# Two deformable convolutions turned from unrolled half images into a loop over tile rows, with smaller patches in the second

## The reference, cut to what matters

```
off1 = conv2d(x, w_off1, b_off1)                      # 18 channels: (dy, dx) of 9 taps
out  = relu(bn(deform_conv(x, off1, w_dc1, stride 1, pad 2, dilation 2)))
off2 = conv2d(out, w_off2, b_off2)
out  = relu(bn(deform_conv(out, off2, w_dc2, 1, 2, 2)) + x)

deform_conv: for every tap (ky, kx) and pixel (r, c)
    ys = r - 2 + 2*ky + dy,   xs = c - 2 + 2*kx + dx
    sample = bilinear value of the image at (ys, xs), zero outside
    out   += w_dc[:, :, ky, kx] @ sample
```

## Time and profile before

| what | us |
|---|---|
| median of 3 runs | 894.47 |
| profiled execution | 889.64 |
| its span | 887.6 |
| PE matmul busy | 728.3 (82%) |
| DVE busy | 484.3 (55%) |
| ACT busy | 417.0 (47%) |

### The profile page before, as it was taken

The page is one execution under the profiler, slowest core; times in us unless marked ns, Lnnn a source line. Parts: engine busy times, 40 slices in busy tenths (PEclk is TensorE's granted clock), DMA queues, the critical chain, the costliest instruction groups (busy, mean ns, idle before and its releaser), DMA issues.

```text
span 887.6 us, 40461 instructions
## 1 busy us (share of the span) xinstructions
PE 728.3 (82%) x18746; PEld 567.3 (64%) x18746; DVE 484.3 (55%) x840; ACT 417.0 (47%) x830; POOL 161.4 (18%) x190
## 2 busy tenths in 40 slices
PE   6787877788767887778788656999999999999546
PEld 2355555566633455555566545999999999998433
DVE  0565554455604645446455564666666666666654
ACT  1665455554315554546544143445445445545442
POOL 7000000000030000000000153343443443341300
PEclk8889878866769798887976578999999999999669
DMA  5400000000004000000000170000000000000002
GB/s 171 82 4 5 4 4 5 5 4 4 5 6 81 4 5 4 4 4 4 5 4 4 29 193 1 1 2 1 0 0 0 0 0 0 0 0 0 0 1 96
DMA packets 7835, 16.58 MB, mean 19 GB/s; under 512 B 1982, under 2 KB 5950, under 8 KB 7286
## 3 DMA queue, kind: packets, MB, share of 16 engines
q1 hardware_dynamic: 7678, 14.21, 6.3%
HBM read 10.34 MB, written 3.87 MB: 16 GB/s over the span
## 4 chain that ended last, share of the span: by engine, by line
PE 76%; issue 10%; DVE 6%; ACT 5%; POOL 1%; DMA 1%; SPq 0%; DVEq 0%
PE banks L227 20%; PE banks L145 14%; PE banks L696 7%; PE banks L680 7%; PE banks L726 6%; PE banks L458 4%; PE banks L737 4%; PE banks L716 3%; PE banks L691 2%; PE banks L180 2%; PE banks L166 2%; PE banks L707 2%; ACT hx L273 1%; DVE norm_stats L629 1%; ACT hy L278 1%
## 5 line engine op out<-in xcount | busy, mean ns | idle before, releaser
L227 PE MATMUL banks<-s,y 32*64 32x96 f32 (+9 forms) x10752 | 191.1, 268 | 66.0 <-issue 65.9
L318 DVE TENSOR_TENSOR s<-hy,hx 128x384 f32<-128x384 f32 (+3 forms) x336 | 144.4, 476 | 183.4 <-PE banks L227 181.8
L227 PEld LDWEIGHTS banks<-s,y 32*64 32x64 f32 x10752 | 160.2, 154 | 109.9 <-issue 100.2
L145 PE MATMUL banks<-w_dc,tiled 64*32 64x192 f32 x3584 | 130.2, 412 | 20.3 <-issue 13.7
L268 ACT COPY y<-banks 128x384 f32<-128x384 f32 x192 | 81.8, 484 | 114.0 <-PE banks L145 114.0
L145 PEld LDWEIGHTS banks<-w_dc,tiled 64*32 64x32 f32 x3584 | 74.3, 131 | 53.8 <-issue 26.6
L794 ACT COPY hy<-banks 128x512 f32<-128x512 f32 x64 | 37.6, 588 | 116.7 <-PE banks L726 116.7
L278 ACT ACTIVATE hy<-banks 128x512 f32<-128x512 f32 (+2 forms) x144 | 72.9, 583 | 38.4 <-PE banks L180 38.3
L898 POOL TENSOR_TENSOR y<-y,stats 128x1024 f32<-128x1024 f32 x33 | 62.8, 1902 | 142.2 <-DVE stats L839 142.2
L273 ACT ACTIVATE hx<-banks 128x384 f32<-128x384 f32 x144 | 61.4, 505 | 31.8 <-PE banks L166 23.9
L680 PE MATMUL banks<-src,s 128*128 (+1 forms) x560 | 75.0, 279 | 1.1 <-ACT src L617 1.1
(11 more groups left out here) (137 smaller groups left out, 876.9 us busy)
## 6 DMA issues: line engine op xcount, KB each, us to landing
src<-in_x_dram SPq DMA_DIRECT2D x4, 578.0 KB, 5.5
y<-in_w_dram SPq DMA_DIRECT2D x1, 2080.0 KB
off<-in_w_dram SPq DMA_DIRECT2D x2, 1024.0 KB
out_dram<-tokens SPq DMA_DIRECT2D x4, 512.0 KB, 2.6
offsets_dram<-tokens SPq DMA_DIRECT2D x32, 54.0 KB
off<-offsets_dram SPq DMA_DIRECT2D x16, 108.0 KB
w_dc<-in_w_dc_dram SPq DMA_DIRECT2D x2, 288.0 KB, 6.0
y<-in_w_attn_dram SPq DMA_DIRECT2D x1, 512.0 KB, 4.9
```

The costliest lines, as they stand in the source:

```text
L145: last = nc.tensor.matmul(m.ps[32 * j:32 * j + 32, FIRST_BANK + (count + g) % RING, (col % 2) * 192:(col % 2) * 192 + 192], m.tiled[rows, ...
L227: last = nc.tensor.matmul(out[:, r0:r0 + strip.n, first:first + width], m.y[32 * j:32 * j + 32, g, (s // 3) % 2 * Y_SLOTS + strip.slot, co ...
L318: nc.vector.tensor_tensor(dst, hy, hx[:, :, r0:r0 + strip.n, :], ALU.mult).then_inc(cv.s_ready, 1)
```

## The change

- TensorE's sampler becomes a loop (`pe.Fori(0, TR)`) of 8 iterations, one per source tile row. The body has the 9 taps written out; each with one x item, one y item, 32 sample matmuls, and in six taps (0, 4, 5, 6, 7, 8) one w item behind the samples. The other engines stay unrolled in the same order. Waits in the loop are against `i * constant + constant`, and the coordinate matmuls read `m.off_flat` at an address that moves with i.
- The four output banks hold 12 rows (OUT_ROWS). After a tile row ScalarE copies the rows that are new (`copied`), VectorE adds the overlap to the sums in `tokens` (`added`), TensorE clears the banks (4 matmuls of 384 columns) and goes on. Batch norm and ReLU are applied per tile row (`rows_act`, `rows_dve`), the last two rows at the end (`last_act`, `last_dve`).
- Column hats are computed for the 4 new rows only and kept in `hx_near` for the next tile row; one x item is 4 matmuls (128 and 64 or 32 columns), all 128 partitions deep (`near_sel`), one y item is 2 matmuls of 8 or 6 rows of 32.
- A w item is emptied by one copy of 768 elements in place of two of 384; x and y items likewise by one activation.
- GpSimd stages one tile row at a time (`stage_pool`, 4 copies a row) and cuts the whole image only for the far sampler.
- `REACHES = [2, 1]`: patches of 8x12 in the first convolution and 6x10 in the second, whose flag is compared with 1.
- VectorE makes s in two instructions per tap: over the old rows (2 * reach) and the 4 new ones. SLOTS goes from 5 to 3.
- Both halves of the offsets are awaited at the sampler's start.

```diff
-REACH = 2
+REACHES = [2, 1]
-SLOTS = 5
+SLOTS, HY_SLOTS = 3, 3
+OUT_ROWS = 12
+FIRST_WEIGHTED = [("w", ky, part, 0) for ky in range(3) for part in range(2)][0:5]
+FIRST_COORDS = [("x", tap, -1) for tap in range(3)] + coords(0) + coords(1) + [("x", tap, -1) for tap in range(3, 6)]
+AHEAD = 2
+STEP_WEIGHTED = {0: (2, 1, 0), 4: (0, 0, 1), 5: (0, 1, 1), 6: (1, 0, 1), 7: (1, 1, 1), 8: (2, 0, 1)}
+def columns_near(nc, m, cv, k, tap, row, n, i=None):
+    _, cols, ahead = window(cv)
+    kx = tap % 3
+    for late in range(2):
+        wide = 2 * cv.reach if late else TILE_COLS
...
+        for g in range(2):
...
+            last = nc.tensor.matmul(dst[:, :, :, TILE_COLS * late:TILE_COLS * late + wide],
+                                    m.near_sel[:, 6 + ((ahead * 3 + kx) * 2 + late) * 2 + g, :], src[:, :, :, 0:wide],
+                                    start=True, stop=True, skip_group_check=True)
+    last.then_inc(cv.filled, 1)
 def sampler_pe(nc, pe, m, cv):
+    for half in range(HALVES):
+        pe.wait_ge(cv.moved[half], MOVES)
+    for k, item in enumerate(FIRST_COORDS, len(FIRST_WEIGHTED)):
...
+    with pe.Fori(0, TR) as i:
+        k = BEFORE_LOOP
+        for t in range(TAPS):
+            later, tap = divmod(t + AHEAD, TAPS)
+            pe.wait_ge(cv.emptied, i * PER_ROW + (k - 1))
+            columns_near(nc, m, cv, k, tap, new_rows(cv, tap) + TILE_ROWS * later, TILE_ROWS, i)
+            k += 1
+            pe.wait_ge(cv.emptied, i * PER_ROW + (k - 1))
+            rows_near(nc, m, cv, k, tap, first_row(cv, tap) + TILE_ROWS * later, i)
+            k += 1
+            if t == 0:
+                pe.wait_ge(cv.copied, i + COPIED_FROM)
+                pe.wait_ge(cv.added, i + (ADDED_FROM - 1))
+                pe.wait_ge(cv.cleared, 1)
+                for bank in range(PAIRS):
+                    nc.tensor.matmul(m.ps[:, bank, 0:OUT_ROWS * W], m.zeros[:, 0:P], m.zeros[:, 0:OUT_ROWS * W],
+                                     start=True, stop=True, skip_group_check=True)
+            if t in STEP_WEIGHTED:
+                pe.wait_ge(cv.emptied, i * PER_ROW + (k - 1))
+                if STEP_WEIGHTED[t] == (0, 0, 1):
+                    pe.wait_ge(cv.staged, i * PAIRS + 2 * PAIRS)
...
+            pe.wait_ge(cv.s_ready, i * (2 * TAPS) + (2 * t + 2))
+            for col in range(TC):
+                first, width, skip = near_columns(cv, col, kx)
+                for j in range(4):
+                    for g in range(2):
...
+                        last = nc.tensor.matmul(out[:, r0:r0 + n, first:first + width],
+                                                m.yk[32 * j:32 * j + 32, ky, g, col, kx * C:(kx + 1) * C],
+                                                s_rows(m, cv, t)[32 * j:32 * j + 32, :, g, at:at + width],
+                                                start=False, stop=True, skip_group_check=True)
+            last.then_inc(cv.sampled, 1)
+            if t in STEP_WEIGHTED:
+                weighted_near(nc, m, cv, k, *STEP_WEIGHTED[t][0:2])
+                k += 1
 def sampler_act(nc, act, m, cv):
...
+    for tile_row in range(TR):
+        for t in range(TAPS):
+            if t == 2 and tile_row >= 2:
+                cv.rows_act(act, tile_row - 2)
+            for kind, *_ in step_items(tile_row, t):
+                if t == TAPS - 1 and kind == "w" and tile_row < TR - 1:
+                    act.wait_ge(cv.sampled, TAPS * (tile_row + 1))
+                    first, n = (TILE_ROWS, 2 * TILE_ROWS) if tile_row == 0 else (2 * TILE_ROWS, TILE_ROWS)
+                    at = TILE_ROWS * (tile_row - 1) + first
+                    nc.scalar.copy(sum_rows(m, at, n), out_rows(m, first, n)).then_inc(cv.copied, 1)
+                item_act(nc, act, m, cv, k)
+                k += 1
+    cv.last_act(act)
 def sampler_dve(nc, dve, m, cv):
...
+    for n in range(TR * TAPS):
+        if n + 1 < TR * TAPS:
+            hats(n + 1)
...
+        if n % TAPS == 0 and n // TAPS >= 2:
+            below = n // TAPS - 1
+            dve.wait_ge(cv.sampled, n)
+            dve.wait_ge(cv.copied, COPIED_FROM + below + 1)
+            first = TILE_ROWS * (below - 1)
+            nc.vector.tensor_tensor(sum_rows(m, first, 2 * TILE_ROWS), sum_rows(m, first, 2 * TILE_ROWS),
+                                    out_rows(m, 0, 2 * TILE_ROWS), ALU.add).then_inc(cv.added, 1)
+            cv.rows_dve(dve, below - 1)
+        weights(n)
...
-                nc.vector.tensor_scalar(far_flag[0:1, cv.k:cv.k + 1], far[0:1, cv.k:cv.k + 1], REACH, None,
+                nc.vector.tensor_scalar(far_flag[0:1, cv.k:cv.k + 1], far[0:1, cv.k:cv.k + 1], cv.reach, None,
                                         ALU.is_ge).then_inc(cv.flag_ready, 1)
```

More of the change, by code:

```diff
@@ L55, in near_strips @@
[L55 to L71, removed]
@@ L74, in near_columns @@
[L74 to L125, removed]
@@ new lines, in step_items @@
+def step_items(tile_row, tap):
+    items = coords(TAPS * tile_row + tap + AHEAD)
+    if tap in STEP_WEIGHTED:
+        ky, part, later = STEP_WEIGHTED[tap]
+        items.append(("w", ky, part, tile_row + later))
+    return items
+BEFORE_LOOP = len(FIRST_WEIGHTED) + len(FIRST_COORDS)
+PER_ROW = sum(len(step_items(0, tap)) for tap in range(TAPS))
+ITEMS = FIRST_WEIGHTED + FIRST_COORDS + [
+    item for tile_row in range(TR) for tap in range(TAPS) for item in step_items(tile_row, tap)]
+EMPTIED_AT = {item: k + 1 for k, item in enumerate(ITEMS)}
@@ new lines, in tile_rows, with rows_near @@
+def tile_rows(off_flat, first, n, i):
+    room = (TAPS * PIX + OFF_TAIL - first) // W * W
+    return off_flat[:, first:first + room].rearrange("p (r c) -> p r c", c=W)[:, bass.ds(i * TILE_ROWS, n), :]
+def rows_near(nc, m, cv, k, tap, row, i=None):
+    n = window(cv)[0]
+    first = tap * PIX + row * W
+    for g in range(2):
+        src = m.off_flat[:, first:first + n * W] if i is None else tile_rows(m.off_flat, first, n, i)
+        dst = slot_banks(m, k)[:, g, 0:n * W]
+        last = nc.tensor.matmul(dst if i is None else dst.rearrange("p (r c) -> p r c", c=W),
+                                m.near_sel[:, tap // 3 * 2 + g, :], src, start=True, stop=True, skip_group_check=True)
+    last.then_inc(cv.filled, 1)
@@ L148, in weighted_pe @@
                 if col % 2 and j == 3:
[L149 to L169, removed]
@@ L172, in rows_pe @@
[L172 to L185 removed]
+                    last.then_inc(cv.all_filled, 1)
@@ new lines, in columns_all @@
+def columns_all(nc, pe, m, cv, count, h, tap, col):
+    pe.wait_ge(cv.all_emptied, count - RING + 2)
+    for g in range(2):
+        rows = group_rows(g, 1)
+        nc.tensor.matmul(m.ps[:, FIRST_BANK + (count + g) % RING, :],
+                         m.sel[rows, (TILE_COLS * col - 2 * (tap % 3) + 4) // 2, :],
+                         m.off[rows, tap, HALF_ROWS * W * h:HALF_ROWS * W * (h + 1)],
+                         start=True, stop=True, skip_group_check=True).then_inc(cv.all_filled, 1)
@@ new lines, in rows_all @@
+def rows_all(nc, pe, m, cv, count, h, tap, tile_row):
+    pe.wait_ge(cv.all_emptied, count - RING + 2)
+    for g in range(2):
+        rows = group_rows(g, 0)
+        nc.tensor.matmul(m.ps[:, FIRST_BANK + (count + g) % RING, :],
+                         m.sel[rows, (TILE_ROWS * tile_row - 2 * (tap // 3) + 4) // 2, :],
+                         m.off[rows, tap, HALF_ROWS * W * h:HALF_ROWS * W * (h + 1)],
+                         start=True, stop=True, skip_group_check=True).then_inc(cv.all_filled, 1)
@@ L334 @@
-ALL_SLOTS = 2
-class Row:
-    def __init__(self, tile_row, h):
-        self.tile_row, self.first, self.n, self.at = tile_row, HALF_ROWS * h, HALF_ROWS, 0
 def all_pe(nc, pe, m, cv):
-    count, n = FIRST_ITEMS, 0
+    count, n = 0, 0
     pe.wait_ge(cv.tiled, TILED)
-    pe.wait_ge(cv.moved[1], MOVES)
+    pe.wait_ge(cv.emptied, len(FIRST_WEIGHTED))
+    for half in range(HALVES):
+        pe.wait_ge(cv.moved[half], MOVES)
     for h in range(HALVES):
```

523 lines of the change are left out of this document (316 added, 207 removed).

## The result

| us | before | after |
|---|---|---|
| median of 4 runs each, same chip | 894.77 | 982.59 |
| all runs | 892.66 to 900.74 | 969.90 to 985.65 |
| profiled execution | 889.64 | 981.66 |
| span | 887.6 | 979.6 |
| sampler 1 | 213.8 | 227.1 |

The changed kernel is slower: 1.092 times the time of before, 95% interval 1.080 to 1.104. Executions of either kernel fall into a faster and a slower state, and every ratio in this document compares fast runs with fast runs, so it is not quite the quotient of two medians. The forecast was 882 us, 840 to 932.

What follows compares the result with a forecast made beforehand. Instruction supply to TensorE was taken to bound both samplers. With the loop kept, sampler 1 at +3 and sampler 2 at -15 us gave 878 for the profiled execution, 882 us as median; range 840 to 932.

Steps and rivals of the forecast that it cites:

- The bound of before: Both unrolled samplers run at the pace of instruction supply to TensorE, about 256 instructions per 3.7 us.
- I take that it stays: The new sampler loop body, about 1,710 instructions, stays in TensorE's instruction memory in both samplers, without refetching each row.
- The price of a lost loop: Rival, chance 0.27: the body doesn't stay; 7.5 transfers of 3.7 us make 27.8 us a row in both samplers, 931.
- The row if it stays: One tile row of a kept loop at clock 1.0: 25.2 us in the first convolution, 23.5 in the second.
- The wait: In six taps a row, y of the next tap waits for ScalarE's copy of the w item: 1.17 us.
- VectorE's lag: In the three plain taps VectorE is later than TensorE: 2.2 us a row, 0.9 in the second convolution.
- the row change: Between tile rows TensorE waits 1.0 us for ScalarE's copy and VectorE's addition and s; the clear lies inside.
- the rival of a low clock: Rival, chance 0.17: the body stays but the clock stays at 0.80; rows of 28.0 and 25.2 us, 911.
- The price of the lower level: A row wholly at clock 0.5 takes 33.5 us in the first convolution and 28.2 in the second.
- The head: Start of each sampler: 9.5 us, including 1.5 us for the second half of the offsets; 10 and 11 with first-iteration supply.
- The sum: Sampler 1 217 us against 213.8, sampler 2 202 against 216.8; together -12 us on the profiled execution, 878.
- the waits overlap better: Rival, chance 0.13: half of the 1.17 us wait falls away, clock stays up; rows 21.7 and 20.0 us, 817.

Runs made afterwards that it cites:

- e8: Kernel before with each sample matmul over half of its rows, same number of instructions; 892.53 us, 0.996 times before.
- e11: e4 with the item order in four of nine taps changed to x, w, y; 858.84 us, 0.956 times before.
- e5: Changed kernel with TensorE's loop over tile rows unrolled, order and waits the same; 938.40 us, 1.048 times before.
- e2: Changed kernel with 64 small zero matmuls before the first sampler and 94 before the second, exchanging the loops' block positions; one run, 962.29 us.
- e1: Changed kernel with 30 small zero matmuls (60 instructions) on TensorE before the second sampler; 913.88 us, 1.020 times before.
- e4: e1 with each w item filled ahead of its tap's samples, a small zero matmul carrying the slot wait; 877.23 us, 0.981 times before.

## Why the prediction was wrong

**The bound of before: right.** e8 shows that it isn't the columns, and e11 that TensorE can take such instructions faster than they came.

**"I take that it stays": the step that failed.** I compared sizes, 1,710 against 1,340 and 14,461, and gave both samplers one answer. The size was right (1,718), and in sampler 1 it stayed. What decides lies in something that I wrote and then left out of the sum. The Trainium skill ("Runtime: NRT & Kernel Launch", Instruction fetch mechanics) gives TensorE 2,048 instructions in blocks of 256; that 8 blocks touched and one ahead would be 9 was my own step from there. 1,718 instructions fill 6.7 blocks, so they touch seven only from positions 0 to 74, 75 of 256. The table agrees but for its edge: kept in about that stretch, and 9 transfers a row where lost, eight blocks and one more. Worked out as a chance, each sampler stayed with about 0.3, and both with far less than the 0.73 that I left for it. The positions are fixed by the code ahead of each loop. The trace of before couldn't show them; a count of the new kernel's code, which I made only afterwards, would have.

**The price of a lost loop: too low.** The rival had 7.5 transfers of 3.7 us, 27.8 us a row; measured were 9 transfers and 36 us. Supply in straight-line code hides behind other waits (e5: 27.1 and 28.6 us a row). A return into a lost block doesn't: nothing runs for 4 us, the next block isn't ahead yet either (1.4 us), and the waits for ScalarE (25.5 us from 345 to 590 us) come on top. Not all of the 36 us is supply. In e2 the lost sampler had a clock of 0.88 over its rows and rows of 33.4 us, 7 more than kept. In the kernel after the lost sampler had 0.63, and the clears took 526 ns against 326; against the kept row of e1 at 0.64 (31.2 us) its rows cost 5 us more. So I estimate 5 to 7 us a row for the refetching and the rest for the clock. Each sampler ran at a lower clock lost than kept (the first at 0.87 and 0.96, the second at 0.63 and 0.84 to 0.92), but that the stalls pull it down isn't shown.

**The row if it stays: mechanism right, size 5 and 8% low.** 25.2 us were worked out and 26.4 measured at clock 1.00; in the second convolution 23.5 and 25.5 (e1, 382.3 to 407.8 us, clock 1.00). The timeline of the kernel after shows one w step, PE alone:

```profile
154.66 0.39 PE L149 MATMUL banks<-off,near_sel 128*128 x2 [0.82 <-ACT y L238]
155.04 0.99 PE L214 MATMUL banks<-s,y 32*64 32x80 f32 x64
155.96 0.88 PE L111 MATMUL banks<-w_dc,stage 64*32 64x192 f32 x32
156.77 0.35 PE L130 MATMUL banks<-off,near_sel 128*128 x4
157.94 0.28 PE L149 MATMUL banks<-off,near_sel 128*128 x1 [0.81 <-ACT y L238]
```

From y to y 3.28 us against 2.99. The wait was exact: x to y is 1.17 us (156.77 to 157.94). What was low is each group of matmuls, start to start: y 0.38 (0.30), samples 0.92 (0.80), w 0.81 (0.72). I had scaled bursts of 128 and 64 down to 64 and 32 and added 0.05 for the change of shape; 0.17 and 0.14 were needed. Two terms were too high and hid part of this: VectorE's lag is there in two taps a row, but with 1.3 us a row (8.4 us in 6.7 rows) and not 2.2, and at the row change nothing waits for VectorE, so only the clears cost time, 0.65 us (3.93 from y to y there) and not 1.0.

**Clock: about as forecast in sampler 1, open in sampler 2.** Sampler 1 runs at 0.96 with 74% of PE busy and waits of 0.8 us. A kept sampler 2 runs at 0.92 (e1) and 0.84 (e2), and its single rows fall to 0.63 (e2's first between two returns, 30.1 us) without a stall for supply. So the rival of a low clock is wrong for the first sampler and in part right for the second, and what sets the level there is open. The price of the lower level was too low as well: 28.2 us were forecast for a row wholly at 0.5, and rows at a mean of 0.64 took 31.2. In sampler 2 of the kernel after, from 343.20 to 345.90 us at a clock of 0.50, 64 samples of 60 columns took 1.17 us from start to start (343.27 to 344.44) where 0.80 were forecast.

**The head: mis-sized.** 1.5 us were set for the second half of the offsets. The waits from 28 to 80 us, after:

```profile
PE banks L130 <- DMA off<-offsets_dram: 8.8, 1, 8.8
```

8.8 us in one wait; the whole first row took 42.2 us against 26.4 for the others, 15.8 more where 10 were forecast. In e4 and e11 it is still 7.5 and 7.9 us, now nearly 1% of the time. A version that waits for the second half later wasn't tried, since the first x items read across both halves.

**The sum.** Sampler 1 was to take 217 us and took 227: 4 in the rows, 6 in the head. Sampler 2 was to take 202 and took 290; in e1, where it is kept, 222. So of the 88 us that sampler 2 was off, 68 belong to the lost loop with its lower clock and 20 to rows and head. Even with both loops kept (e1) the change is about 2% slower than before (the interval, 1.0005 to 1.040, just leaves out none): it gets rid of the supply bound and takes on a wait for ScalarE (32.8 us in 176). At the old pace of 3.7 us per 256 the 1,718 instructions of a row would have come in 24.8 us; the row's own chain takes 26.4. A gain could come only from a shorter chain, as in e4 and e11. So without the lost loop the forecast of a gain of 1.4% would have failed too. The rival "the waits overlap better" (817) holds for no kernel as changed, but it names what e4 and e11 did by another order, and 859 is how far that went.

## What to carry to other kernels

A loop on TensorE that nearly fills the instruction memory is kept or lost by the position of its first instruction, as this one was: count its blocks with the position, not by its size alone, leave some tens of instructions of margin (my count was five off in one sampler, and past the edge rows were lost by degrees), look at the instruction queue between two returns for every loop separately, and move a lost one with a few instructions ahead of it, or shorten the body until every position fits. Where the bound was instruction supply, the loop only uncovers the next wait; look at once for who waits for whom in the new body and put an independent item between, since here that order was worth 55 us (914 to 859), while the change with both loops kept and the old order was no gain on the kernel before (and about 3% on the same code written out, 1.020 against 1.048).

## What was not expected of the hardware

- A loop of 1,718 TensorE instructions ran seven iterations without one transfer at positions 10 to 80, and with 9 transfers an iteration at 166 and 232.
- In e11 a kept body of 1,729 instructions took 22.0 us, 79 instructions a us; supply brings 256 in 3.7 us, 69 a us. So supply is not far below the pace of this whole body with its waits; a burst of samples alone runs about twice as fast as supply (1.80 us for 256 instructions). A lost loop is worse than unrolled code: 33.4 against 27.1 us a row in the first sampler, 36 against 28.6 in the second.
- Halving the rows of every sample matmul changed the time of the supply-bound kernel by 0.4%, although its samplers' mean granted clock was 0.66 in the profiled run, against 0.80 before.
- A kept row without any transfer ran at a mean clock of 1.00 and of 0.64 within one kernel (e1), 25.5 and 31.2 us.
